# Local attention with the value products of a tile three tiles behind its scores, instead of two

## What is computed

```python
x = x + _L0_attn_a_ref(_layernorm(x), w_qkv, b_qkv)      # local attention: 16 heads of 16 features, blocks of 32
x = x + _L0_ffn_ref(_layernorm(x), ...)
x = x + _L0_attn_b_ref(_layernorm(x), ...)               # differential attention over all 1024 tokens
x = x + _L0_ffn_ref(_layernorm(x), ...)

def _attention(q, k, v, head_dim):
    scores = jnp.einsum('bghqd,bghkd->bghqk', q, k) / head_dim ** 0.5
    w = jax.nn.softmax(scores, axis=-1)
    return jnp.einsum('bghqk,bghkd->bghqd', w, v)
```

## Time and profile before

| what | value |
|---|---|
| median of the three runs shown (lowest to highest) | 8106.93 us (8104.33 to 8115.15) |
| the profiled execution's own time | 8101.32 us |
| its span, first to last instruction | 8099.7 us |
| busy: PE, DVE, ACT, POOL | 93%, 85%, 77%, 45% of the span |
| mean granted TensorE clock | 0.96 of full speed |

### The profile page before, as it was taken

One profiled execution on the slowest core, in us unless ns is written; L12 is line 12 of the kernel. 1 busy time (PEld: TensorE's weight loads), 2 busy tenths in 40 slices (PEclk: granted clock), 3 DMA queues, 4 the chain that ended last, 5 costly groups with the idle time before them and its releaser, 6 DMA issues. The chain is left out here.

```text
span 8099.7 us, 182418 instructions
## 1 busy us (share of the span) xinstructions
PE 7531.0 (93%) x72640; PEld 3385.8 (42%) x72640; DVE 6895.6 (85%) x8962; ACT 6196.6 (77%) x11486; POOL 3637.2 (45%) x5187
## 2 busy tenths in 40 slices
PE   6999989999899998999989999899998999989999
PEld 4344443444434444344443444434444344444444
DVE  5899768997689976899768997699976999768997
ACT  3699756997569975699756997569975699756996
POOL 4366333662336623366234662346623466134661
PEclk8999989999889999999998999999999999988999
DMA  0122101220011200121001210022200222002210
GB/s 31 50 46 46 27 12 53 44 48 23 12 55 43 47 23 12 55 47 43 23 12 56 48 43 21 12 58 46 47 21 8 63 45 46 25 1 63 47 44 25
DMA packets 604272, 298.88 MB, mean 37 GB/s; under 512 B 486966, under 2 KB 528438, under 8 KB 603382
## 3 DMA queue, kind: packets, MB, share of 16 engines
q1 hardware_dynamic: 603388, 286.86, 14.5%
HBM read 123.83 MB, written 67.37 MB: 24 GB/s over the span
## 5 line engine op out<-in xcount | busy, mean ns | idle before, releaser
L1485 DVE TENSOR_REDUCE mall<-ps 128x1 f32<-128x1024 f32 x4096 | 4670.8, 1217 | 87.7 <-PE ps L1419 84.8
L1576 ACT ACTIVATE work<-ps 128x512 f32<-128x512 f32 x8192 | 4311.6, 602 | 164.2 <-PE ps L1435 39.6
L1451 PE MATMUL ps<-work,vbuf 128*32 128x256 f32 x32768 | 2624.7, 392 | 23.8 <-ACT hh L1583 3.3
L1435 PE MATMUL ps<-qop,kop 51*128 51x256 bf16 x16384 | 2560.1, 273 | 8.7 <-ACT work L1576 7.5
L1419 PE MATMUL ps<-kop,qop 48*128 48x512 bf16 x8192 | 2539.2, 386 | 31.2 <-DMA kop<-scratch 18.6
L1435 PEld LDWEIGHTS ps<-qop,kop 51*128 51x128 bf16 x16384 | 1183.7, 94 | 1886.2 <-ACT work L1576 1596.3
L1451 PEld LDWEIGHTS ps<-work,vbuf 128*32 128x32 f32 x32768 | 661.9, 108 | 926.5 <-issue 592.1
L252 POOL TENSOR_TENSOR rstd<-rstd,nhalf 128x8 f32<-128x8 f32 x64 | 109.4, 1709 | 1637.9 <-DVE rstd L246 1637.9
L1510 POOL TENSOR_TENSOR mall<-mall 128x8 f32<-128x8 f32 x1024 | 214.2, 209 | 1252.1 <-DVE mall L1485 1211.9
L444 POOL TENSOR_TENSOR hh<-work,hmask 128x1024 f32<-128x1024 f32 x256 | 520.3, 2061 | 445.6 <-POOLq L1681 328.1
L1538 POOL TENSOR_TENSOR work<-work,none 128x16 f32<-128x16 f32 x224 | 650.9, 2906 | 18.1
(11 more groups left out here) (179 smaller groups left out, 8752.0 us busy)
## 6 DMA issues: line engine op xcount, KB each, us to landing
qop<-scratch SPq DMA_DIRECT2D x512, 64.0 KB
scratch<-work SPq DMA_DIRECT2D x32, 768.0 KB, 4.1
scratch<-hh SPq DMA_DIRECT2D x32, 768.0 KB, 3.7
kop<-scratch SPq DMA_DIRECT2D x256, 96.0 KB
vbuf<-in_x SPq DMA_DIRECT2D x9, 2048.0 KB, 8.4
qop<-scratch SPq DMA_DIRECT2D x512, 32.0 KB
kop<-scratch SPq DMA_DIRECT2D x256, 64.0 KB
qop<-mT SPq DMA_DIRECT2D x1024, 3.0 KB
```

Source lines behind the costliest of these rows:

```text
L1435: mm = pe.matmul(ps[:, bank, part * HQ:(part + 1) * HQ], kop[r:r + KM, s, i, (t + part) * P:(t + part + 1) * P], qop[r:r + KM, s, i, quart ...
L1451: mm = pe.matmul(ps[VW * i:VW * (i + 1), OB, kept], vp[:, b, t, (G * gl + i) // 2, :], prob[:, u % PS, i, cols], start=t == 0, stop=t == T ...
L1485: v.tensor_reduce(mall[:, m // CUT % 2, to, col:col + 1], ps[:, b:b + NB, :].rearrange("p b n -> p (b n)"), AX.X, ALU.max).then_inc(s_mr, 1)
L1576: act.activation(prob[:, u % PS, hl, :], ps[:, EB[slot % len(EB)], :], ACT.Exp, scale=scale).then_inc(s_ex, 1)
```

## The change

The value products of a tile move one step later in TensorE's stream: at step t TensorE issues `values(t - 3)` instead of `values(t - 2)`, and the loop has one step more. No instruction is added or removed, and the other engines' streams are the same, row for row.

```diff
-                    for t in range(TT + 2):
+                    for t in range(TT + 3):
                         if t < TT:
                             scores(t)
-                        if t >= 2:
-                            values(t - 2)
+                        if t >= 3:
+                            values(t - 3)
                         if t < 2:
                             v_piece(0, 2 * t)
                             v_piece(0, 2 * t + 1)
...
```

## The result

The changed kernel takes 8019.94 us (median of five runs, 7996.41 to 8056.29) against 8106.93 us before: a ratio of 0.9899, 95% interval 0.988 to 0.9918. The forecast was 8031 in a range of 7998 to 8073.

What follows compares the result with a forecast made beforehand. VectorE's maximum was taken to wait for TensorE's scores, queued behind value products waiting for placing. Per pair 6.6 + 6.0 - 3.2 = 9.4, say 9.5 us, 76 us in all, gave 8031 us, range 7998 to 8073.

Steps and rivals of the forecast that it cites:

- What bounds the stage: Local-attention stage: TensorE idles before value products until ScalarE's placing, delaying scores and VectorE's maximum; 16.8 us per pair at stake.
- Step 2: Scores(3) start at 1091.8 instead of 1097.59, the piece taking 3.63 us instead of 5.01; VectorE's whole 4.17 us wait goes.
- Steps 3 to 5: TensorE never waits and is the bound at 5.29 us a step; 6.6 us gained by the scores of tile 6.
- Steps 6 to 15: VectorE's work is the bound; 6.0 us of idle time goes, ten multiplications cost 3.2 us more.
- ScalarE and the end: ScalarE's keep has 1.1 us of cover, and tile 15 waits for its placing as before; both cost nothing.
- L469's idle time: Sign in the changed profile: VectorE's wait for scores at its maximum falls from 204.7 us to about 75.
- 4.0 us of slack: VectorE's spare time in steps 3 to 5, where TensorE is the bound; longer multiplications there cost nothing.
- The mean of L486: Sign in the changed profile: VectorE's multiplication rises from a mean of 0.884 to about 1.1 us.
- The one in which the multiplication loses nothing more: Rival: VectorE's multiplication gets no longer, 12.6 us per pair gained, 8006 us; chance 0.22.
- The one in which ScalarE takes the wait over: Rival: keep and placing wait for the later value products, so time stays at 8107 us; chance 0.05.
- The random: Rival: multiplications meet GpSimd's products at random, 0.8 us each in ten steps, 4.6 us per pair gained, 8070 us; chance 0.19.
- the slower one: Rival: every multiplication starts just behind a GpSimd product's start, losing 1.54 us; 3.4 us per pair slower, 8134 us; chance 0.04.

Runs made afterwards that it cites:

- e4: Against the kernel before: value products still two tiles behind, but the projection piece of each of steps 2 to 9 issued ahead of them; ratio 0.9934 to before.
- e6: Against the change: VectorE's inverse of the sums moved behind the next tile's shift, still kept in SBUF; ratio 0.9957 to the kernel before.
- e9: Against the change: inverse of the sums in the PSUM bank of its own tile's scores, VectorE's order kept, TensorE waiting longer; 7992.54 us, ratio 0.987 to before.
- e5: Against the change: inverse of the sums moved behind the next tile's shift and written into the PSUM bank just read; ratio 0.9898 to the kernel before.

## Why the prediction was right

*What bounds the stage.* Right. TensorE standing still before the value products held back scores, and through them VectorE; e4 shows it without any change of distance.

*Step 2.* Right, and in the number a little lucky: scores(3) were put at 1091.8 - 1072.0 = 19.8 us after the table load and came at 1083.04 - 1063.28 = 19.8. There scores(2) happened to come 0.4 us earlier in the stage than before (1078.41 - 1063.28 = 15.1 us instead of 15.5), and the scores took 1.00 us (1078.41 to 1079.41) instead of 0.65; the median over the pairs is 20.05. The whole 4.17 us of idle time went, and the piece took 3.70 us at a granted clock of 1.00 (1079.41 to 1083.04), which is the 2.4 GHz that was taken. From scores(2) to scores(3) are 4.63 us instead of 10.06: 2.70 of idle time, 1.35 of value products that no longer stand there and 1.31 by which the piece was slow are gone. That nothing below would change at 1.2 GHz was wrong, though: with TensorE the bound in steps 3 to 5, the 1.4 us would have reached scores(6) and maximum(6).

*Steps 3 to 5.* Right that TensorE is the bound there, but these steps gained almost nothing: 5.29 us a step was put, 5.50 measured (1083.04, 1088.55, 1094.05). The 0.65 us for the scores came from a row with a gap behind it; with value products directly behind them the next instruction starts 0.89 us after them (1083.04 to 1083.93). The rows of before already said so: scores(3), (4) and (5) start at 1097.59, 1103.09 and 1108.80, 5.50 and 5.71 us apart. Of the 6.6 us, 5.8 lay in step 2 (1097.59 to 1091.8) and 0.8 here; 0.2 were gained here in the median, and 5.7 in all.

*Steps 6 to 15.* Right in kind; here a term was mis-sized. Of the 6.0 us of idle time 0.36 are left; counted from the start of each total to the start of the maximum behind it, steps 7 to 15 are 6.1 us shorter. The ten multiplications were to cost 3.2 us more and cost 1.4 (9.19 us instead of 7.83). So 4.9 us were gained instead of 2.8. Of the bounds, 0 and 1.54 us each, the upper one was a little low: the longest multiplication of e6, 2.41 us, is 1.73 above 0.68. The middle was a guess at a phase, and the phase of the change happens to be a good one: in four steps running the multiplication takes about 0.82 us.

*ScalarE and the end.* Right: L553 waits 13.3 us over the run, 13.2 before, and the end of the stage is unchanged in length: 15.1 to 15.3 us from the total behind step 15 to the last residual addition (L497), 15.1 to 15.2 before.

*The sum.* 9.5 us a pair were forecast; the stage gave 10.6, 5.7 instead of 6.6 up to maximum(6) and 4.9 instead of 2.8 behind it. So the forecast is as close as it is partly by luck: one part was put too high and the other too low. The pair distance of 994.3 us, as forecast, is partly chance, since the rest of the pair was 1.1 us longer in that profile. L469's idle time was put at about 75 us and is 99.5. The prediction there forgot its own 4.0 us of slack, which is a wait of VectorE for scores in steps 3 to 5; it measures 1.03 + 2.13 = 3.2 us in each pair. The mean of L486, put at 1.1 us, is 1.06, partly by chance too: half of the 2.9 us that the multiplications cost more in a stage falls in steps 3 and 4, where it lies in the slack.

*The rivals.* The one in which the multiplication loses nothing more is out by the mean of L486, 1062 ns instead of 884, and not by the time: its 8006 us lie inside the range of the change's runs. The one in which ScalarE takes the wait over is out by the time and by L553. The random and the slower one differ from the forecast only by phase, and e6 reached a mean of 1.35 us. Even there the stage was 1.1 us shorter than before (91.11 against 92.25), because the gain of steps 2 to 5 stands.

## What to carry to other kernels

In an engine's queue that is worked through in order, look at what is ready behind an instruction that waits; one more tile between producer and consumer, or other work put ahead of the waiting instruction, are two cures for the same stall, and the distance is enough once the engine that is to use what stands behind the wait no longer finds it late. A gain in such a loop has to be followed to the engine that is the bound next, step by step: in e9 shorter multiplications brought time only where VectorE, and not TensorE, was the bound. And before counting on two engines side by side, look at the scatter of one operation's duration: here the spread from 0.68 to 2.2 us was a second wait, which no list of waits shows.

## What the runs showed of the hardware that was not expected

A VectorE multiplication with two SBUF operands and GpSimd's products hold each other up in both directions: 0.68 to 2.4 us for the one, 1.89 to 2.35 us for the other, and with one operand in PSUM both are nearly constant (686 to 689 ns and 1891 to 1904 ns in e5). What it costs is a matter of phase: the same instructions in a slightly different order took 17.0 us a stage (the change) or 21.6 (e6).
